# First attention of a two-layer Flamingo block: on TensorE, the scores of even slots are issued in front of the maxima

## Chip, cores and metric

One core of one Trainium2 chip runs the whole kernel. The time is device microseconds from launch to end, the median of three executions.

## What is computed

Two layers follow one another on 16 batches of 112 rows of 256 features: cross attention to 375 context rows and then a mixture of experts, twice. The change lies in the first cross attention, which has 16 heads of 16 features:

```python
q = jnp.einsum('btd,hdk->bhtk', tgt, Wq) + bq[None, :, None, :]
k = jnp.einsum('bsd,hdk->bhsk', src, Wk) + bk[None, :, None, :]
v = jnp.einsum('bsd,hdk->bhsk', src, Wv) + bv[None, :, None, :]
scores = jnp.einsum('bhtk,bhsk->bhts', q, k) * scale
weights = jax.nn.softmax(scores, axis=-1)
out = jnp.einsum('bhts,bhsk->bhtk', weights, v)
```

`tgt` is the normalised x (16 x 112 x 256), `src` the context (16 x 375 x 256).

## The kernel before

The attention takes a batch of 112 query rows at a time. Each of its 16 heads is computed twice. First comes a product of queries by keys whose only use is its row maximum ("maxima", two matmuls for a pair of heads, L400); VectorE reduces it (L782). After four pairs the maxima are turned by TensorE (`turn_maxima`, L410), negated in two parts by VectorE (L787, L789) and put by DMA as two extra rows under the queries. Then the product is computed again, keys by queries, with the maximum already subtracted ("scores", six matmuls, L344). ScalarE takes the exponential of it (L642). TensorE multiplies by the values ("values", L356, four heads at a time), ScalarE copies that result out of PSUM (L637), TensorE turns it back (`turn_values`, L364), and VectorE divides by the sums ("finish", L795 and L797).

A batch is eight slots s = 0 to 7, and each engine has its own `emit` that writes its instructions slot by slot; engines take their instructions in order and meet only at semaphores. In slot s of batch b, TensorE does maxima s of batch b + 1, values in odd slots, and scores s - 2 of batch b (scores 6 and 7 of batch b - 1 in slots 0 and 1). In even slots it also does one of four projections of batch b + 3: keys in slots 0 and 2 (six matmuls), values in slots 4 (twelve) and 6 (six), all recorded at L51. Even slots end with `turn_values`. Batches 13 and 14 have no such projection left, but parts of the output projection; batch 15 has no maxima.

Four waits matter here. Maxima s waits until VectorE has reduced maxima s - 1, because both use the same two PSUM banks (`psMX`). Even scores wait for ScalarE's copy of the values result (`o_copied`), because that result (`psPV`) lies in the first PSUM bank of the even scores. `turn_maxima` waits for an earlier finish of VectorE (`o_free`). The `turn_values` of slots 0 and 4 waits until VectorE has negated the maxima (`turn_free`). VectorE's order in a slot is: reduction; the negation in slots 0 and 4; the low part of the keys (L754) in slots 1 and 3; finish in odd slots.

Of the kernel before, what the change touches and what calls it, by code (L numbers as in the profile page):

```python
# [37 lines left out]
def at_least(engine, sem, value):  # L38

    if isinstance(value, int) and value <= 0:  # L40
        return
    engine.wait_ge(sem, value)
# [68 lines left out]
def ring(b):  # L111
    return Ring(b // 4, b % 4)


def l0_attention(nc, k, a, xd):

    with ExitStack() as ctx:
# [96 lines left out]
        def tail_group(b):  # L214

            return b.b - TAIL if b is not None and isinstance(b.b, int) and b.b >= TAIL else None
# [16 lines left out]
        def scores_at(p, b, s):  # L233

            return (p, s + NJ - LAG) if s < LAG else (b, s - LAG)

        def values_at(p, b, s):

            return (p, 2 + s // 2) if s < 4 else (b, s // 2 - 2)

        def turned_at(p, b, s):

            return (p, 1 + s // 2) if s < 6 else (b, s // 2 - 3)

        def task_at(ws, s):

            if len(ws) == 2:
                return ws[s // 4], s % 4
            return (ws[0], s // 2) if ws and s % 2 == 0 else (None, None)
# [17 lines left out]
        with nc.Block(no_gpsimd_drain=True) as block:  # L267
# [63 lines left out]
            def _(pe):  # L331
                def scores(b, j):

                    if j % JJ == 0:
                        pe.wait_ge(c_in[j // JJ][b.odd], b.half * 64 + 64)
                    at_least(pe, exp_done, b.b * NJ + (j - 1))
                    if j % 2 == 0:
                        at_least(pe, o_copied, b.b * NH + j // 2 - 1)
                    if b.b == 0 and j == 0:
                        pe.wait_ge(v_free, 2 * 3)  # L340
                    for c in range(SC):
                        for h in range(2):
                            side = slice(SIDE * h, SIDE * h + DOT)
                            last = nc.tensor.matmul(psST[:C, j % 2, h, c * T:(c + 1) * T],  # L344
                                                    stkK[side, b.slot, j % JJ, j // JJ, c * C:(c + 1) * C],
                                                    stkQ[side, j % JJ, bass.ds(b.b, 1), j // JJ, :].rearrange("p o q -> p (o q)"),
                                                    start=True, stop=True)
                    last.then_inc(st_full, 1)

                def values(b, g, exps):  # L350

                    pe.wait_ge(exp_done, exps)
                    for c in range(SC):
                        for q in range(QH):
                            h = QH * g + q
                            last = nc.tensor.matmul(psPV[VW * q:VW * (q + 1), :], V[:, b.slot, c, h, :],  # L356
                                                    Pf[:, h // 2 % PB, h % 2, c * T:(c + 1) * T], start=c == 0, stop=c == SC - 1)
                    last.then_inc(pv_full, 1)

                def turn_values(b, g):  # L360

                    pe.wait_ge(o_copied, b.b * NH + g + 1)
                    at_least(pe, o_free, b.b * NH + g)
                    nc.tensor.transpose(k.ps[:T, 6, P:2 * P], oT[:], k.ident[:]).then_inc(o_full, 1)  # L364
# [27 lines left out]
                def maxima(n, j):  # L392

                    if j == 0:
                        pe.wait_ge(k_sp[n.slot], sp_count(n.slot, n.quarter + 1))
                        pe.wait_ge(k_pool[n.slot], pool_count(n.slot, n.quarter + 1))
                    at_least(pe, mx_red, n.b * NJ + j - (1 if n.b == 0 else 0))
                    for h in range(2):
                        side = slice(SIDE * h, SIDE * h + KEYS)
                        last = nc.tensor.matmul(maxima_of(n, j)[:T, h, :S],  # L400
                                                stkQ[side, j % JJ, bass.ds(n.b, 1), j // JJ, :].rearrange("p o q -> p (o q)"),
                                                stkK[side, n.slot, j % JJ, j // JJ, :], start=True, stop=True)
                    last.then_inc(mx_full, 1)

                def turn_maxima(n, half):

                    pe.wait_ge(mx_red, n.b * NJ + JJ * (half + 1))
                    at_least(pe, turn_free, 2 * n.b + half)
                    at_least(pe, o_free, n.b * NH - (3 if half else 5))
                    nc.tensor.transpose(psT[:HH, :], mx[:, n.odd, half].rearrange("p h j -> p (h j)"), k.ident[:T, :T]).then_inc(turn_full, 1)  # L410

                def turn_rows(g, t):

                    pe.wait_ge(o_free, GB * NH * (g + 1))
                    if t == 0 and g == 0:
                        pe.wait_ge(v_free, 2 * B)
                    elif t == 0:
                        pe.wait_ge(y_used, GB * g)
                    elif g < LAST:
                        pe.wait_ge(a_lo, KD * g + 1)  # L420
                    for i in range(GB):
                        last = nc.tensor.transpose(psA(g, t)[:, i * T:(i + 1) * T],
                                                   attn[:, GB * g + i, t * P:(t + 1) * P], k.ident[:T, :T])
                    last.then_inc(a_full, 1)

                def project_rows(n):

                    g, i = n // GB, n % GB
                    if i == 0:
                        pe.wait_ge(w_lo, 4)  # L430
                        pe.wait_ge(a_lo, KD * g + KD)
                    elif g < LAST:
                        pe.wait_ge(y_used, n)
                    three_products(nc, psY(n), [(aT[0][:, g % 2, t, i * T:(i + 1) * T], aT[1][:, g % 2, t, i * T:(i + 1) * T])
                                                for t in range(KD)],
                                   [(wo[0][:, t, :], wo[1][:, t, :]) for t in range(KD)]).then_inc(y_full, 1)
# [44 lines left out]

                def emit(p, b, n, ws, x, l):
                    for s in range(NJ):
                        if n is not None:
                            maxima(n, s)
                        if b is not None and s == 0:
                            turn_maxima(b, 1)
                        of, j = scores_at(p, b, s)
                        row, g = values_at(p, b, s)
                        if row is not None and s % 2 == 1:  # L490
                            values(row, g, row.b * NJ + NJ if of is None else of.b * NJ + j)
                        if of is not None:
                            scores(of, j)
                        if n is not None and s == 4:
                            turn_maxima(n, 0)
                        w, t = task_at(ws, s)
                        if w is not None:
                            (keys if t < 2 else vals)(w, t % 2)
                        o = tail_group(b)
                        if o is not None and s in (0, 2):  # L500
                            turn_rows(o, s // 2)
                        if o is not None and s >= 4:
                            project_rows(GB * o + s - 4)
                        row, g = turned_at(p, b, s)
                        if row is not None and s % 2 == 0:
                            if s == 0 and b is not None:
                                pe.wait_ge(turn_free, 2 * b.b + 2)
                            if s == 4 and n is not None:
                                pe.wait_ge(turn_free, 2 * n.b + 1)
                            turn_values(row, g)  # L510
                    if n is not None and n.b in (GB - 1, Q_TURN - 1):
                        pe.wait_ge(rest_q, 16 * (len(Q_POOL) + (0 if n.b == GB - 1 else len(Q_PIECES))))
                        pe.wait_ge(act_q, 16 * len(Q_ACT))

                emit(None, None, ring(0), (ring(1), ring(2)), None, None)
                for b in range(B + 1):
                    p, b, n, w = (ring(b + d) if 0 <= b + d < B else None for d in (-1, 0, 1, 3))
                    emit(p, b, n, (w,) if w else (), None, None)
# [2139 lines left out]
```

## Time and profile before

| | |
|---|---|
| median of three executions | 891.08 us (890.73 to 892.11) |
| profiled execution | 888.89 us |
| its span, first to last instruction | 886.9 us |
| TensorE busy, of the span | 82% |
| VectorE busy, of the span | 67% |
| ScalarE busy, of the span | 52% |

The profile comes from one execution. The first attention lies in the first third of it: batches 2 to 12 of it run at an even pace between 86.62 us and 237.87 us, 13 and 14 up to 267.47 us. A TensorE row gives the start of a matmul and its modelled end, so the distance between starts is the better measure of what an instruction costs the ones behind it.

### The profile page before, as it was taken

The numbers are of one execution on the slowest core, as the hardware profiler recorded it, in microseconds if no ns is written. First come the engines' busy times: TensorE is split into PE (matmuls) and PEld (weight loads), VectorE is DVE, ScalarE is ACT, GpSimd is POOL, SyncE is SP. The second block draws the span as 40 slices with busy tenths as digits, with TensorE's granted clock in tenths as the row PEclk, the third lists the DMA queues.
The fourth block names the chain that finished last, engine by engine and source line by source line (L and its number), as shares of the span: only waits on it lengthen the run. The fifth ranks groups of instructions, "written<-read, shape, count | busy, mean of one in ns | idle before, by whom it ended". The sixth has DMA issues, their size and how long they took to land. (4 is left out here: it accounts for less than half of the span.)

```text
span 886.9 us, 21023 instructions
## 1 busy us (share of the span) xinstructions
PE 726.0 (82%) x6871; PEld 548.3 (62%) x6871; DVE 594.9 (67%) x1432; ACT 464.7 (52%) x953; POOL 458.5 (52%) x592
## 2 busy tenths in 40 slices
PE   3789999999987598989999998478798379997820
PEld 2456666666665498988777777367686246665510
DVE  5566777777785669884445542678867356667766
ACT  3546666766655468673333331344454247776632
POOL 5788788798600438881000002665833518655555
PEclk9879999999999579999999998797979689999975
DMA  6326444442300428764222223785521214323233
GB/s 174 93 71 148 112 112 118 122 108 74 81 14 2 144 60 295 244 208 129 85 83 79 84 73 89 205 229 166 146 70 44 77 35 139 96 81 95 84 92 104
DMA packets 87662, 98.94 MB, mean 112 GB/s; under 512 B 17260, under 2 KB 77132, under 8 KB 87564
## 3 DMA queue, kind: packets, MB, share of 16 engines
q1 hardware_dynamic: 63468, 66.10, 25.3%
q0 software_dynamic: 16432, 24.66, 10.3%
q10 hardware_dynamic: 7664, 6.89, 2.6%
q8 instruction: 60, 0.98, 0.5%
q14 instruction: 38, 0.31, 0.1%
HBM read 61.03 MB, written 24.38 MB: 96 GB/s over the span
## 5 line engine op out<-in xcount | busy, mean ns | idle before, releaser
L782 DVE TENSOR_REDUCE a_mx<-ps 112x2 f32<-112x750 f32 x128 | 120.2, 939 | 49.9 <-PE ps L400 48.0
L672 POOL DMA_DIRECT2D a_stkK<-a_KS x248 | 119.3, 489 | 19.2 <-issue 14.8
L642 ACT ACTIVATE a_Pf<-ps 125x672 f32<-125x672 f32 x128 | 90.0, 729 | 11.2 <-PE ps L344 9.9
L51 PE MATMUL ps<-f_w2hi,f_hh 128*128 (+1 forms) x292 | 80.3, 275 | 4.0 <-issue 2.8
L51 PE MATMUL ps<-f_w2lo,f_hh 128*128 (+1 forms) x292 | 80.2, 275 | 0.0
L51 PE MATMUL ps<-f_w2hi,f_hl 128*128 (+1 forms) x292 | 80.2, 275 | 0.0
L1841 POOL MEMSET a_half<- 112x2 f32 x1 | 0.1, 94 | 143.7 <-POOLq L88 143.7
L1547 DVE CAST f_hh<-ps 128x512 bf16<-128x512 f32 x41 | 28.4, 692 | 64.4 <-PE ps L1283 64.4
L2453 POOL TENSOR_TENSOR f_rl<-f_rf,f_rh 128x512 bf16<-128x512 f32 x34 | 39.5, 1161 | 59.8 <-DVE f_rh L2521 59.3
L2397 ACT ACTIVATE f_rf<-ps,f_ln 128x128 f32<-128x128 f32 x136 | 54.4, 452 | 25.7 <-PE ps L2348 25.7
L1207 POOL DMA_INDIRECT f_xd<-xn,pos x32 | 54.4, 1700 | 22.9 <-issue 22.9
L51 PE MATMUL ps<-f_w1hi,f_xgThi 128*128 x150 | 57.3, 382 | 0.6 <-DVE f_xgTlo L2502 0.6
L51 PE MATMUL ps<-f_w1hi,f_xgTlo 128*128 x150 | 57.4, 382 | 0.0
L51 PE MATMUL ps<-f_w1lo,f_xgThi 128*128 x150 | 57.4, 382 | 0.0
L400 PE MATMUL ps<-a_stkK,a_stkQ 48*112 48x375 bf16 x256 | 48.6, 374 | 9.9 <-DMA a_stkK<-a_KS 5.4
L1552 DVE TENSOR_TENSOR f_hl<-ps,f_hh 128x512 bf16<-128x512 f32 (+1 forms) x57 | 45.3, 796 | 9.8 <-ACT f_hh L1402 8.9
L356 PE MATMUL ps<-a_Pf,a_V 125*32 125x112 f32 x1536 | 50.6, 265 | 1.4 <-ACT a_Pf L642 1.3
L1388 ACT ACTIVATE f_xgThi<-ps 128x256 bf16<-128x256 f32 x41 | 15.7, 384 | 66.1 <-PE ps L1266 66.1
L344 PE MATMUL ps<-a_stkQ,a_stkK 50*125 50x112 bf16 x768 | 47.2, 228 | 1.2 <-DMA a_stkQ<-a_cneg 0.8
L51 PE MATMUL ps<-f_w2hi,f_rh 128*128 x136 | 37.4, 275 | 8.8 <-POOL f_rl L2453 7.8
L344 PEld LDWEIGHTS ps<-a_stkQ,a_stkK 50*125 50x125 bf16 x768 | 34.2, 134 | 16.0 <-issue 12.0
L356 PEld LDWEIGHTS ps<-a_Pf,a_V 125*32 125x32 f32 x1536 | 35.0, 110 | 13.0 <-issue 8.5
(392 smaller groups left out, 2270.5 us busy)
## 6 DMA issues: line engine op xcount, KB each, us to landing
a_raw<-F_w SPq DMA_DIRECT2D x22, 512.0 KB
f_xg<-f_xd SPq DMA_DIRECT2D x75, 128.0 KB
f_yd<-f_yo SPq DMA_DIRECT2D x75, 128.0 KB
f_raw<-F_w SPq DMA_DIRECT2D x14, 512.0 KB
a_ctxF<-ctxT SPq DMA_DIRECT2D x16, 375.0 KB, 3.5
a_cR<-ctx SPq DMA_DIRECT2D x16, 375.0 KB
a_stkK<-a_KS POOLq DMA_DIRECT2D x248, 23.4 KB, 2.0
f_xd<-a_zero ACTq DMA_DIRECT2D x13, 384.0 KB, 3.2
```

The costliest lines, as they stand in the source:

```text
L51: ins = nc.tensor.matmul(out, l, r, start=first and i == 0, stop=last and i == len(steps) - 1)
L344: last = nc.tensor.matmul(psST[:C, j % 2, h, c * T:(c + 1) * T], stkK[side, b.slot, j % JJ, j // JJ, c * C:(c + 1) * C], stkQ[side, j % JJ ...
L356: last = nc.tensor.matmul(psPV[VW * q:VW * (q + 1), :], V[:, b.slot, c, h, :], Pf[:, h // 2 % PB, h % 2, c * T:(c + 1) * T], start=c == 0, ...
L400: last = nc.tensor.matmul(maxima_of(n, j)[:T, h, :S], stkQ[side, j % JJ, bass.ds(n.b, 1), j // JJ, :].rearrange("p o q -> p (o q)"), stkK[ ...
L642: nc.scalar.activation(Pf[:, j % PB], psST[:C, j % 2, :, 0:SC * T], ACT.Exp, scale=DH ** -0.5).then_inc(exp_done, 1)
L672: pool.dma_start(stkK[SIDE * h + DH * a:SIDE * h + DH * (a + 1), w.slot, jj], KS[2 * DH * jj + DH * h:2 * DH * jj + DH * (h + 1), w.odd, p ...
L782: nc.vector.reduce_max(mx[:, n.odd, j // JJ, :, j % JJ], maxima_of(n, j)[:T, :, :S], AX).then_inc(mx_red, 1)
L1207: nc.gpsimd.indirect_dma_start(out=xd, out_offset=bass.IndirectOffsetOnAxis(pos[:, i, b:b + 1], 0), in_=k.xn[:, b, :], in_offset=None, bou ...
L1547: nc.vector.tensor_copy(like_hidden(s, hh), turned_hidden(s)).then_inc(h_hi, 1)
L1552: tt(like_hidden(s, hl), turned_hidden(s) if s.shared is None else hidden(s), like_hidden(s, hh), ALU.subtract).then_inc(h_lo, 1)
L2397: nc.scalar.activation(rf[:, t % 2, i, :], k.ps[:, 2 + t % 2, i * P:(i + 1) * P], ACT.Relu, bias=ln[:, 1, bass.ds(e, 1), i], scale=ln[:, 0 ...
L2453: nc.gpsimd.tensor_tensor(rl[:, t % 2], rf[:, t % 2], rh[:, t % 2], ALU.subtract).then_inc(r_lo, 1)
```

## The change

Only TensorE's order changes. In slots 0, 2, 4 and 6 the scores, with their waits, are issued first, ahead of the maxima and, in slot 0, ahead of `turn_maxima`. Odd slots keep the order maxima, values, scores.

```diff
                 def emit(p, b, n, ws, x, l):
                     for s in range(NJ):
+                        of, j = scores_at(p, b, s)
+                        row, g = values_at(p, b, s)
+                        if of is not None and s % 2 == 0:
+                            scores(of, j)
                         if n is not None:
                             maxima(n, s)
                         if b is not None and s == 0:
                             turn_maxima(b, 1)
-                        of, j = scores_at(p, b, s)
-                        row, g = values_at(p, b, s)
                         if row is not None and s % 2 == 1:
                             values(row, g, row.b * NJ + NJ if of is None else of.b * NJ + j)
-                        if of is not None:
+                        if of is not None and s % 2 == 1:
                             scores(of, j)
```

On TensorE, at the end of slot 5 and the start of slot 6 of batch 1 (every later batch repeats it), the kernel before has the odd scores, then the maxima, then the even scores, then the projection:

```order
284 L344 MATMUL ps<-a_stkQ,a_stkK 125x112 [waits a0_expdone]
285 L344 MATMUL ps<-a_stkQ,a_stkK 125x112 x5
286 L400 MATMUL ps<-a_stkK,a_stkQ 112x375 [waits a0_mxred]
287 L400 MATMUL ps<-a_stkK,a_stkQ 112x375
288 L344 MATMUL ps<-a_stkQ,a_stkK 125x112 [waits a0_ocopied,a0_expdone,a0_cin11]
289 L344 MATMUL ps<-a_stkQ,a_stkK 125x112 x5
290 L51 MATMUL ps<-a_wv_hi,a_ctxH 125x256 [waits a0_vfree]
```

The changed kernel has at the same place:

```order
284 L344 MATMUL ps<-a_stkQ,a_stkK 125x112 [waits a0_expdone]
285 L344 MATMUL ps<-a_stkQ,a_stkK 125x112 x5
286 L344 MATMUL ps<-a_stkQ,a_stkK 125x112 [waits a0_ocopied,a0_expdone,a0_cin11]
287 L344 MATMUL ps<-a_stkQ,a_stkK 125x112 x5
288 L400 MATMUL ps<-a_stkK,a_stkQ 112x375 [waits a0_mxred]
289 L400 MATMUL ps<-a_stkK,a_stkQ 112x375
290 L51 MATMUL ps<-a_wv_hi,a_ctxH 125x256 [waits a0_vfree]
```

Two scores now stand one behind the other, and the maxima stand behind the wait for ScalarE's copy (`a0_ocopied`). At the start of slot 0 of a batch (here batch 2), before:

```order
303 L400 MATMUL ps<-a_stkK,a_stkQ 112x375 [waits a0_mxred,a0_kinpool3,a0_kinsp3]
304 L400 MATMUL ps<-a_stkK,a_stkQ 112x375
305 L410 MATMUL ps<-ident,a_mx 8x112 [waits a0_ofree,a0_turnfree,a0_mxred]
306 L344 MATMUL ps<-a_stkQ,a_stkK 125x112 [waits a0_ocopied,a0_expdone]
307 L344 MATMUL ps<-a_stkQ,a_stkK 125x112 x5
```

and after:

```order
303 L344 MATMUL ps<-a_stkQ,a_stkK 125x112 [waits a0_ocopied,a0_expdone]
304 L344 MATMUL ps<-a_stkQ,a_stkK 125x112 x5
305 L400 MATMUL ps<-a_stkK,a_stkQ 112x375 [waits a0_mxred,a0_kinpool3,a0_kinsp3]
306 L400 MATMUL ps<-a_stkK,a_stkQ 112x375
307 L410 MATMUL ps<-ident,a_mx 8x112 [waits a0_ofree,a0_turnfree,a0_mxred]
```

Here both the maxima and `turn_maxima` have gone behind the scores.

## Rows read from the trace of the kernel before

**Rows 1.** The page: TensorE's granted clock in 40 slices of the span

```profile
PEclk9879999999999579999999998797979689999975
```

**Rows 2.** Windows: length, busy PE, PEld, DVE, ACT, POOL, PEclk, DMA, GB/s

```profile
86.62:224.30 137.68, 129.95 (x1961) 88.27 (x1962) 105.34 (x221) 93.15 (x172) 116.70 (x215) 1.00 0.42 109
237.87:267.47 29.60, 25.86 (x394) 17.95 (x395) 23.98 (x52) 15.89 (x29) 1.88 (x4) 1.00 0.10 26
```

**Rows 3.** Waits in those ten batches: us in total, times, longest

```profile
DVE a_mx L782 <- PE ps L400: 25.4, 44, 0.9
PEld ps L400 <- DVE a_mx L782: 5.7, 20, 0.4
```

**Rows 4.** Timeline of TensorE, batch 6 (slot 0 at 141.62): start, us

```profile
141.62 0.37 PE L400 MATMUL ps<-a_stkK,a_stkQ 48*112 48x375 bf16 x2
...
143.54 0.27 PE L364 MATMUL ps<-ident,a_oT 128*112 128x128 f32 x1
143.75 0.37 PE L400 MATMUL ps<-a_stkK,a_stkQ 48*112 48x375 bf16 x2
144.04 0.78 PE L356 MATMUL ps<-a_Pf,a_V 125*32 125x112 f32 x24
144.75 0.38 PE L344 MATMUL ps<-a_stkQ,a_stkK 50*125 50x112 bf16 x6
...
146.97 0.37 PE L400 MATMUL ps<-a_stkK,a_stkQ 48*112 48x375 bf16 x2
...
149.43 0.26 PE L410 MATMUL ps<-ident,a_mx 112*8 112x112 f32 x1 [0.50 <-DVE xn L797]
...
151.04 0.37 PE L400 MATMUL ps<-a_stkK,a_stkQ 48*112 48x375 bf16 x2
...
152.44 0.37 PE L400 MATMUL ps<-a_stkK,a_stkQ 48*112 48x375 bf16 x2
152.65 0.33 PE L344 MATMUL ps<-a_stkQ,a_stkK 50*125 50x112 bf16 x6
152.91 0.32 PE L51 MATMUL ps<-a_wv_hi,a_ctxH 128*125 128x256 bf16 x1
...
153.85 0.37 PE L400 MATMUL ps<-a_stkK,a_stkQ 48*112 48x375 bf16 x2
...
155.35 0.37 PE L400 MATMUL ps<-a_stkK,a_stkQ 48*112 48x375 bf16 x2
```

**Rows 5.** Timeline of VectorE, the same batch

```profile
142.03 0.94 DVE L782 TENSOR_REDUCE a_mx<-ps 112x2 f32<-112x750 f32 x1
...
143.17 0.26 DVE L789 SCALAR_TENSOR_TENSOR a_cneg<-ps,a_cneg 8x112 bf16<-8x112 f32 x1
...
145.98 0.93 DVE L782 TENSOR_REDUCE a_mx<-ps 112x2 f32<-112x750 f32 x1
...
149.26 0.94 DVE L782 TENSOR_REDUCE a_mx<-ps 112x2 f32<-112x750 f32 x1
...
152.85 0.94 DVE L782 TENSOR_REDUCE a_mx<-ps 112x2 f32<-112x750 f32 x1
```

**Rows 6.** Timeline, batch 15 (no maxima): values, their copy, next even scores

```profile
269.19 0.78 PE L356 MATMUL ps<-a_Pf,a_V 125*32 125x112 f32 x24
...
270.04 0.26 ACT L637 ACTIVATE a_oT<-ps 128x112 f32<-128x112 f32 x1 [0.23 <-PE ps L356]
...
270.44 0.38 PE L344 MATMUL ps<-a_stkQ,a_stkK 50*125 50x112 bf16 x6 [0.17 <-ACT a_oT L637]
```

**Rows 7.** Timeline of TensorE, batch 0: scores, then maxima

```profile
68.79 0.38 PE L344 MATMUL ps<-a_stkQ,a_stkK 50*125 50x112 bf16 x6
69.01 0.33 PE L400 MATMUL ps<-a_stkK,a_stkQ 48*112 48x375 bf16 x2
```

**Rows 8.** Timeline of TensorE, batch 1, slot 2

```profile
75.65 0.37 PE L400 MATMUL ps<-a_stkK,a_stkQ 48*112 48x375 bf16 x2
...
76.87 0.32 PE L344 MATMUL ps<-a_stkQ,a_stkK 50*125 50x112 bf16 x4 [0.85 <-DMA a_stkQ<-a_cneg]
```

## Prediction

> **What bounds it now.** I began with the windows, because the change touches only the first attention. In the ten batches from 86.62 us TensorE's rows cover 129.95 of 137.68 us and VectorE's 105.34 [rows 2], with TensorE's clock at its full level. So TensorE looks like the limit with VectorE well behind. The chain of waits says more: VectorE stands 25.4 us idle in front of reductions because the maxima have not been computed, and TensorE waits for the reductions as well, 20 times in 80 slots [rows 3]. The two hand one pair of PSUM banks back and forth, maxima, reduction, maxima, and a late link of that loop is late for good unless something else ends later anyway. The timeline of one batch then tells which of the two ends last in each slot [rows 4, 5].
>
> I count from an odd maxima M(o) = 0. The next even maxima stand at 1.40 (151.04 to 152.44) or, in slot 0, at 1.50 (153.85 to 155.35) [rows 4]. From a maxima to its reduction's start it is 0.41 (141.62 to 142.03 and 152.44 to 152.85), and from a reduction's start to the maxima that it releases 0.99 or 1.00 (145.98 to 146.97, 152.85 to 153.85) [rows 4, 5]. The loop's own pace is therefore 1.40 us a slot: the 1.40 above is just this loop, so TensorE, done with the odd scores, waited a little for VectorE.
>
> **What the new order costs.** No instruction is added or removed, and VectorE, ScalarE and the DMA queues keep their order. What moves is the time at which the even maxima start, through two terms.
>
> First, the even scores now come straight behind the odd scores, and so run into the wait for ScalarE's copy of the values result. Before, the maxima covered it. Batch 15 has no maxima and shows the bare sequence: values at 269.19, copy 270.04 to 270.30, even scores at 270.44, which is 1.25 behind the values, 0.17 of it named as waiting for the copy [rows 6]. Values start 0.29 behind M(o) (143.75 to 144.04) [rows 4]; taken as 0.30, the even scores stand at 1.55. Before they stood at 1.61 (151.04 to 152.65) [rows 4]. So going first brings the scores only 0.06.
>
> Second, the maxima follow the scores. The spacing of that pair is seen free of a wait once, 0.22 [rows 7], which puts the even maxima at 1.77, against 1.40 and 1.50: later by 0.37 in slots 2, 4 and 6 and by 0.27 in slot 0. The upper bound of this spacing is 0.40, what is left of 1.40 after 0.29 and the 0.71 from values to odd scores (144.04 to 144.75) [rows 4]; there the maxima also waited for VectorE, so it is surely too much. I take 0.22.
>
> TensorE's own work does not change to speak of. The pair and what follows cost 0.21 + 0.26 before (152.44, 152.65, 152.91) [rows 4]; now 0.22 plus 0.29, the spacing from maxima to a full-array matmul, taken from maxima to values. That is 0.04 more.
>
> What a late even maxima costs differs by slot.
> - Slot 2: its reduction started at 145.98, 2.23 behind M(1) = 143.75 [rows 4, 5], because VectorE was still at the keys and at finish. The late maxima allow 1.77 + 0.41 = 2.18. VectorE still ends last. For TensorE itself the next maxima come at 1.77 + 0.29 + some 1.2 for projection and turn, 3.25 against 3.22 (143.75 to 146.97): +0.03. (The 1.2 is 3.22 less 1.61, 0.26 and about 0.15 of waiting.)
> - Slot 4: the reduction started at 149.26, 2.29 behind M(3) = 146.97 [rows 4, 5]; 2.18 is still in time. The turn of the maxima, which waits 0.50 for finish [rows 4], stays at 149.43, since the late maxima fall into that wait. 0.
> - Slot 6: no such cover, because VectorE has no keys in slot 5. Maxima 1.77, reduction 2.18, slot 7's maxima 3.17 to 3.18, against 2.81 (151.04 to 153.85) [rows 4]: +0.36.
> - Slot 0: from its maxima to the turn of values it is 1.92 (141.62 to 143.54) [rows 4], and that turn waits for reduction and negation (142.03 to 143.43) [rows 5]. Both move with the maxima: +0.27. Everything of slot 1 is queued behind that turn.
>
> A steady batch thus loses 0.36 + 0.27 + 0.03 = 0.66 us. There are eleven of them (2 to 12): 7.3 us. Batch 1 has slots 0 and 6 (0.63) and slot 2, where the scores wait for a DMA until 76.87 while the maxima had gone at 75.65 [rows 8]; now they start about 77.1, their reduction 77.5, slot 3's maxima 78.5, against 76.87 + 0.26 + 1.2 = 78.33: about 0.2, with slot 2's own cost 0.3, together 0.9. Batch 0 loses at slot 6 and gains where its maxima waited for VectorE and scores can now fill the wait: an estimate of +0.3. In batches 13 and 14 output projections stand between odd scores and even maxima in slots 6 and 0, and cover part of the copy: I take batch 13's slot 0 in full, 0.27, and half of the other three, 0.5: 0.8 for both. Batch 15 has no maxima: 0. Sum 7.3 + 0.9 + 0.3 + 0.8 = 9.3 us. The experts start behind a barrier at the end of the attention, so nothing later hides it: the profiled 888.89 becomes 898.2. The median before lies 2.2 higher, and becomes 900.4.
>
> Both ends: with a copy wait that costs nothing (scores about 0.25 behind the odd ones, at 1.25) the even maxima stand near 1.47, slot 6 loses 0.07, slot 0 nothing, and the sum is about 1 us. With 0.40 between scores and maxima each even slot is 0.18 later, slots 2 and 4 lose their cover as well, and 0.66 becomes about 1.25 a batch, 16 to 17 us in all.
>
> **A rule of the skill against this reading.** The Trainium skill, "Perfetto Trace Analysis", section "Identifying the Most-Contended Engine", says that TensorE's matmul busy share misleads and that weight-load busy time is to be set against the occupancy of the others. Rows 2 give 88.27 us of weight load against VectorE's 105.34, so by that rule VectorE is the engine to watch, and it agrees with the loop above. Taken to its end, every delay of a reduction would be paid in full; what that would give is the second rival.
>
> **Rivals.**
> 1. The copy wait is less than batch 15 shows, or VectorE's own lateness covers more slots: +1 to +5 us, 892 to 896. For it: slots 2 and 4 are covered by only 0.05 and 0.11, so small shifts move the balance. Against: batch 15's wait is in the trace, and slot 6 has no cover. 0.13.
> 2. VectorE ends last everywhere: three slots at 0.37 and one at 0.27 are 1.38 a batch, 15.2 over eleven, 2 to 3 more outside: 908.5. For it: the same thin cover. Against: the reductions at 145.98 and 149.26 did not wait for maxima. 0.10.
> 3. The other side, faster: the even maxima's 1.40 is TensorE's own time, not VectorE's, so scores in front fill a gap and nothing waits for the reduction. TensorE's spacing from M(o) to the projection was 1.87; with scores at 1.25, maxima 1.47 and projection 1.76 each even slot gains 0.1, 56 slots 6 us: 885. It decides if even scores come at 1.3 or before. Against: 0.41 + 0.99 is exactly 1.40. 0.06.
> 4. More idle time makes the granted clock fall in the attention. The page's clock digit is 9 from the fourth slice to the twelfth, which is this stretch, also where TensorE is 87% busy [rows 1, 2]. A microsecond at half level costs about as much again; a few such stretches bring 910 or more. 0.04.
> 5. The order hardly matters, within 0.2%, which is also about what a measurement of this kernel can tell from no change: 0.05.
>
> The forecast itself holds 0.62. The likeliest time is 900.4 us; the range 893 to 907.5 takes in most of rival 1 and the upper bound of the spacing, and leaves out rivals 2 to 5 and some of 1. Faster 0.06, same 0.07 (case 5 and the foot of rival 1), slower 0.87.
>
> **What would show it.** In the changed profile: even scores 0.5 to 0.55 behind odd ones, with a wait named for the copy (L637); even maxima near 1.77 behind odd ones; VectorE's idle time in front of reductions up by about 0.6 us a batch; a batch of 14.4 us instead of 13.73 (141.62 to 155.35) [rows 4]; slots 1 to 3 and 3 to 5 as long as before. Even scores at 1.3, or a batch below 13.9, would make the copy term wrong; slots 2 and 4 longer by 0.3 would make the cover wrong; a change of length after the attention would make the barrier argument wrong.

## The result and the profile after

The changed kernel takes 899.89 us (median of 20 executions, 891.34 to 904.91) against 892.18 us (20 executions) of the kernel before: a ratio of 1.0083 with a 95% interval of 1.0066 to 1.0100, or 5.9 to 8.9 us more. The change makes the kernel slower. The forecast was 900.4, 9.3 more than the 891.08 of three executions; measured is a median 7.7 above the 892.18 of twenty. Its profiled execution took 900.16 us, with a span of 898.2, 11.3 more than before.

In the changed kernel the lines of VectorE and ScalarE stand two further down: the reduction is L784, the copy L639, the second negation L791 and finish L799.

The ten batches from batch 2 to batch 11, then a stretch in batch 13 (windows; columns as in the windows of before):

```profile
85.86:228.57 142.71, 127.92 (x1966) 85.29 (x1964) 105.54 (x220) 91.96 (x171) 115.13 (x212) 1.00 0.42 106
245.30:254.80 9.50, 9.49 (x99) 6.33 (x101) 6.42 (x13) 3.87 (x7) 0.00 (x0) 0.50 0.03 6
```

The ten batches took 137.68 us before and take 142.71 now, with about the same work on every engine and TensorE at its full clock level in both [rows 2]. So 0.50 us a batch have come as waiting, not as work. The second row has no counterpart in the windows of before: for 9.5 us in batch 13 TensorE was at its lower level, 1.2 GHz. That is the first part of the difference that the order of instructions does not explain by itself. The page shows it in slice 12:

```profile
PEclk9979999999989669998999999699989688999975
```

The waits of the ten batches (total us, times, longest):

```profile
DVE a_mx L784 <- PE ps L400: 32.0, 60, 1.0
...
PE ps L344 <- ACT a_oT L639: 7.3, 41, 0.7
...
PEld ps L400 <- DVE a_mx L784: 6.2, 20, 0.4
```

VectorE's idle time in front of reductions rose from 25.4 to 32.0 us, and from 44 waits to 60 [rows 3]. TensorE waits for ScalarE's copy in front of 41 of the scores, four a batch and one more.

TensorE's timeline of batch 6 from the maxima of slot 5 to those of slot 7, and behind it slots 0 and 1 of batch 7:

```profile
152.28 0.37 PE L400 MATMUL ps<-a_stkK,a_stkQ 48*112 48x375 bf16 x2
152.58 0.78 PE L356 MATMUL ps<-a_Pf,a_V 125*32 125x112 f32 x24
153.29 0.38 PE L344 MATMUL ps<-a_stkQ,a_stkK 50*125 50x112 bf16 x6
153.84 0.38 PE L344 MATMUL ps<-a_stkQ,a_stkK 50*125 50x112 bf16 x6 [0.17 <-ACT a_oT L639]
154.03 0.35 PE L400 MATMUL ps<-a_stkK,a_stkQ 48*112 48x375 bf16 x2
...
155.41 0.37 PE L400 MATMUL ps<-a_stkK,a_stkQ 48*112 48x375 bf16 x2
...
157.16 0.35 PE L400 MATMUL ps<-a_stkK,a_stkQ 48*112 48x375 bf16 x2
157.44 0.26 PE L410 MATMUL ps<-ident,a_mx 112*8 112x112 f32 x1
...
159.13 0.32 PE L364 MATMUL ps<-ident,a_oT 128*112 128x128 f32 x1 [0.47 <-DVE a_cneg L791]
159.38 0.37 PE L400 MATMUL ps<-a_stkK,a_stkQ 48*112 48x375 bf16 x2
```

The even scores start 0.55 behind the odd ones (153.29 to 153.84), with a wait of 0.17 for the copy. They are 1.56 behind the odd maxima (152.28), 1.55 by the forecast. The maxima follow at 154.03, 1.75 behind the odd ones, 1.77 by the forecast and 1.40 before [rows 4].

VectorE, slots 2, 4, 5, 6 and 7 of the same batch:

```profile
147.23 0.93 DVE L784 TENSOR_REDUCE a_mx<-ps 112x2 f32<-112x750 f32 x1
...
150.51 0.94 DVE L784 TENSOR_REDUCE a_mx<-ps 112x2 f32<-112x750 f32 x1
...
152.69 0.94 DVE L784 TENSOR_REDUCE a_mx<-ps 112x2 f32<-112x750 f32 x1 [0.78 <-PE ps L400]
...
154.42 0.94 DVE L784 TENSOR_REDUCE a_mx<-ps 112x2 f32<-112x750 f32 x1 [0.33 <-PE ps L400]
155.82 0.94 DVE L784 TENSOR_REDUCE a_mx<-ps 112x2 f32<-112x750 f32 x1 [0.47 <-PE ps L400]
```

The reductions of slots 2 and 4, at 147.23 and 150.51, have no wait: VectorE was the later one there, as before. That of slot 6, at 154.42, waits 0.33 for the late maxima and passes the delay on to slot 7 (155.41).

The distances between the starts of maxima, medians over batches 2 to 11, are the most exact measure in this case; where a kernel was profiled twice (before, changed, late_turn), the two agree in each of them to 0.01 us. All kernels of this text in one table (from slot to slot; the last column is the sum, a batch):

| | 0-1 | 1-2 | 2-3 | 3-4 | 4-5 | 5-6 | 6-7 | 7-0 | batch |
|---|---|---|---|---|---|---|---|---|---|
| before | 2.13 | 1.40 | 1.82 | 1.40 | 2.67 | 1.41 | 1.40 | 1.50 | 13.74 |
| changed | 2.11 | 1.74 | 1.48 | 1.77 | 2.30 | 1.74 | 1.39 | 1.74 | 14.27 |
| front_2_4 | 2.12 | 1.74 | 1.48 | 1.77 | 2.30 | 1.41 | 1.41 | 1.50 | 13.73 |
| front_0_6 | 2.11 | 1.40 | 1.82 | 1.41 | 2.67 | 1.74 | 1.39 | 1.74 | 14.27 |
| free_copy_before | 2.31 | 1.41 | 1.81 | 1.41 | 2.67 | 1.40 | 1.49 | 1.50 | 14.00 |
| free_copy_after | 2.21 | 1.41 | 1.81 | 1.43 | 2.65 | 1.41 | 1.49 | 1.50 | 13.90 |
| copy_twice | 2.11 | 1.90 | 1.46 | 1.90 | 2.18 | 1.90 | 1.39 | 1.90 | 14.74 |
| late_turn | 2.13 | 1.41 | 1.82 | 1.40 | 2.18 | 1.63 | 1.41 | 1.50 | 13.48 |
| late_turn_both | 1.73 | 1.57 | 1.82 | 1.41 | 2.17 | 1.64 | 1.41 | 1.50 | 13.25 |
| late_turn_after | 2.11 | 1.74 | 1.48 | 1.77 | 1.94 | 1.74 | 1.39 | 1.74 | 13.91 |

Read it in pairs that begin at an odd slot. From slot 1 to slot 3 it is 3.22 before and after, from 3 to 5 4.07 and 4.07, from 5 to 7 2.81 and 3.13, from 7 to 1 3.63 and 3.85. Slots 2 and 4 lose 0.34 to 0.37 in front of the even maxima and get it all back behind them; slots 6 and 0 do not.

The medians differ by 0.54 a batch, the eleven batches together by 5.7 us and not by 5.9, mainly because batches 3 and 7 were longer than the others already before (13.96 and 14.11) and lose only 0.3 each.

### The profile page after: what moved, and what is told of

Same layout as the page of the kernel before. It is cut to its first block and busy times, and to the rows that moved or that the text cites. A ratio compares the mean times of both kernels' runs of the same rounds, so it can differ in the third digit from the quotient of the medians.

```text
span 898.2 us, 20990 instructions
## 1 busy us (share of the span) xinstructions
PE 723.0 (80%) x6838; PEld 544.4 (61%) x6871; DVE 593.6 (66%) x1432; ACT 463.3 (52%) x953; POOL 460.5 (51%) x592
## 5 line engine op out<-in xcount | busy, mean ns | idle before, releaser
L784 DVE TENSOR_REDUCE a_mx<-ps 112x2 f32<-112x750 f32 x128 | 120.3, 940 | 59.1 <-PE ps L400 58.4
L1209 POOL DMA_INDIRECT f_xd<-xn,pos x32 | 57.0, 1781 | 23.1 <-issue 23.1
L344 PE MATMUL ps<-a_stkQ,a_stkK 50*125 50x112 bf16 x768 | 49.7, 235 | 12.3 <-ACT a_oT L639 9.0
L51 PE MATMUL ps<-f_w1hi,f_xgTlo 128*128 x140 | 54.0, 386 | 1.6 <-DVE f_xgTlo L2504 1.0
L51 PE MATMUL ps<-f_w1lo,f_xgThi 128*128 x140 | 53.4, 382 | 0.5
L356 PE MATMUL ps<-a_Pf,a_V 125*32 125x112 f32 x1536 | 52.7, 273 | 1.3 <-ACT a_Pf L644 1.3
L51 PE MATMUL ps<-f_w1hi,f_xgThi 128*128 x137 | 52.7, 385 | 0.7 <-issue 0.2
L639 ACT ACTIVATE a_oT<-ps 128x112 f32<-128x112 f32 x64 | 16.9, 264 | 59.5 <-PE ps L356 59.5
```

What stands on the lines that cost most here:

```text
L51: ins = nc.tensor.matmul(out, l, r, start=first and i == 0, stop=last and i == len(steps) - 1)
L784: nc.vector.reduce_max(mx[:, n.odd, j // JJ, :, j % JJ], maxima_of(n, j)[:T, :, :S], AX).then_inc(mx_red, 1)
L1209: nc.gpsimd.indirect_dma_start(out=xd, out_offset=bass.IndirectOffsetOnAxis(pos[:, i, b:b + 1], 0), in_=k.xn[:, b, :], in_offset=None, bou ...
```

## Experiments

The theory: the even maxima are held back 0.34 by the scores that wait for ScalarE's copy, and this is paid only in slots 6 and 0, where VectorE has nothing else to be late with. Rivals: the loss is spread over all even slots; or it comes from the pair of scores standing together, not from the copy.

**Only slots 2 and 4 in front.**

```diff
-                        if of is not None and s % 2 == 0:
+                        if of is not None and s in (2, 4):
                             scores(of, j)
...
-                        if of is not None and s % 2 == 1:
+                        if of is not None and s not in (2, 4):
                             scores(of, j)
```

> Only slots 2 and 4 put the scores in front of the maxima; slots 0 and 6 keep the order of before. My theory (the copy wait makes every even maxima 0.34 us late, but in slots 2 and 4 VectorE is still busy with the keys and finish): even maxima there 1.74 behind the odd ones instead of 1.40, and the distances from maxima 1 to 3 and 3 to 5 stay 3.22 and 4.08, so a batch stays at 13.73 and the time within 1.5 us of before. Rival (a late reduction is paid everywhere): both distances 0.34 longer, a batch 14.4, time +8 us or more. Rival (the cost is TensorE's own, of the order scores, scores, maxima): a quarter of the batch's 0.54 in each even slot, so 14.0 a batch and +3.5 us.

Measured: 894.71 us (12 executions) against 894.76 (26), ratio 0.9993 (0.9960 to 1.0025). TensorE's timeline, slots 1 to 4 of batch 6:

```profile
147.09 0.37 PE L400 MATMUL ps<-a_stkK,a_stkQ 48*112 48x375 bf16 x2
...
148.64 0.38 PE L344 MATMUL ps<-a_stkQ,a_stkK 50*125 50x112 bf16 x6 [0.17 <-ACT a_oT L639]
148.83 0.35 PE L400 MATMUL ps<-a_stkK,a_stkQ 48*112 48x375 bf16 x2
...
150.31 0.37 PE L400 MATMUL ps<-a_stkK,a_stkQ 48*112 48x375 bf16 x2
...
152.08 0.35 PE L400 MATMUL ps<-a_stkK,a_stkQ 48*112 48x375 bf16 x2
```

The same wait of 0.17 and the same late maxima (147.09 to 148.83 is 1.74), and slot 3 still comes at 3.22. Two of four even slots can be changed at no price, as the forecast had it.

**Only slots 0 and 6 in front.** The same edit with `(0, 6)`.

> Only slots 0 and 6 put the scores in front. My theory: all of the change's cost is here: maxima 5 to 7 at 3.13 instead of 2.81, maxima 7 to 1 at 3.84 instead of 3.62, a batch 14.27, the time that of the full change, +7 to +9 us over before. Rival (paid everywhere or TensorE's own cost): half of it, a batch 14.0, +4 us.

Measured: 899.21 us (12), ratio 1.0050 (1.0019 to 1.0081). A batch is 14.27, exactly that of the full change. The maxima of slots 5 to 7 of batch 6 lie as in the full change:

```profile
157.59 0.37 PE L400 MATMUL ps<-a_stkK,a_stkQ 48*112 48x375 bf16 x2
...
159.33 0.35 PE L400 MATMUL ps<-a_stkK,a_stkQ 48*112 48x375 bf16 x2
...
160.72 0.37 PE L400 MATMUL ps<-a_stkK,a_stkQ 48*112 48x375 bf16 x2
```

1.74 and then 1.39. So the whole price of a steady batch is in slots 6 and 0; the rival of a spread loss is out. The time itself missed the expectation of +7 to +9: the medians differ by 4.5 us, the interval is 1.7 to 7.2. The 5.7 us of the steady batches lie inside it, but the 7.7 of the full change do not. With the same steady batches the two kernels' rises over before differ by some 3 us, so a median of a dozen executions does not settle the size.

**Without the copy wait, in both orders.** The values result goes to PSUM bank 6, where no scores lie. The even scores then need no wait for the copy. Instead finish, which reads that bank, waits for the copy of the next group, so this costs VectorE something new, and the old order is run with it as the control. The first values of all wait for a negation of the maxima.

```diff
-        psPV = k.ps[:, 0, SC * T:(SC + 1) * T]
+        psPV = k.ps[:, 6, 0:T]
...
-                    if j % 2 == 0:
-                        at_least(pe, o_copied, b.b * NH + j // 2 - 1)
...
                     dve.wait_ge(o_full, b.b * NH + g + 1)
+                    last = isinstance(b.b, int) and b.b == B - 1 and g == NH - 1
+                    dve.wait_ge(o_copied, b.b * NH + g + (1 if last else 2))
```

> The changed order, but the result of values lies in the free columns of PSUM bank 6, so even scores no longer wait for ScalarE's copy (VectorE's finish waits for the copy instead, and the first values wait for the negation). My theory: even scores 0.3 behind the odd ones instead of 0.54, even maxima at about 1.50 instead of 1.74, a batch of 13.8 to 13.95, time +1 to +3 us over before. Rival (the cost comes from the pair's order on TensorE or from three waits in a row, not from the copy): even maxima stay near 1.74 and the time at +7 us or more.

> The same move of the values' result to bank 6 with the order of before: the control for the added waits. My theory: finish starts up to 0.2 us later in slots 5 and 7, which the even maxima cover; a batch 13.7 to 13.85, time -0.5 to +1.5 us against before. Rival (the added waits cost by themselves): +3 us or more, which then has to be taken off the other kernel's time.

Measured in the new order: 900.69 us (9), ratio 1.0084 (1.0050 to 1.0118); in the old order 902.36 (6), 1.0108 (1.0067 to 1.0148). TensorE, slots 5 to 7 in the new order (odd and even scores are now one row of twelve matmuls):

```profile
151.79 0.37 PE L400 MATMUL ps<-a_stkK,a_stkQ 48*112 48x375 bf16 x2
152.09 0.78 PE L356 MATMUL ps<-a_Pf,a_V 125*32 125x112 f32 x24
152.80 0.55 PE L342 MATMUL ps<-a_stkQ,a_stkK 50*125 50x112 bf16 x12
153.20 0.37 PE L400 MATMUL ps<-a_stkK,a_stkQ 48*112 48x375 bf16 x2
...
154.68 0.37 PE L400 MATMUL ps<-a_stkK,a_stkQ 48*112 48x375 bf16 x2 [0.21 <-DVE a_mx L784]
```

The even maxima are back at 1.41 (151.79 to 153.20), although two scores still stand in front of them. So it is the copy wait and not the pair of scores. Without that wait the new order is even the better one: 13.90 a batch against 14.00 of its control. The whole 0.10 is gained between slots 0 and 1 (2.21 against 2.31), where the scores now stand ahead of the waiting `turn_maxima`. It did not make a fast kernel, and here both expectations of the time failed: 5.9 and 7.6 us above before, where +1 to +3 and at most +1.5 had been expected, and the control's batch, 14.00, was expected at 13.85 or less. The wait of finish costs more than I had reckoned: 0.18 between slots 0 and 1 and 0.09 between 6 and 7 in the control, since the turn of the maxima of slot 0, which waits for finish, is in the loop:

```profile
142.74 0.37 PE L400 MATMUL ps<-a_stkK,a_stkQ 48*112 48x375 bf16 x2
143.38 0.26 PE L410 MATMUL ps<-ident,a_mx 112*8 112x112 f32 x1 [0.28 <-DVE xn L799]
```

And from the start of batch 14 to the attention's last turned row it is 35.72 and 34.55 us, against 31.63 before: 4.1 and 2.9 more. The expectation had nothing for this stretch. In the new order 3.4 us of it (260.4 to 263.8) were at the lower clock level, in the old order none; in both the last turns wait up to 1.02 us for finish. With 1.4 and 2.6 in batches 2 to 12 it accounts for 5.5 us of the 5.9 and of the 7.6 by which the two kernels stand above the 894.76 of before. The rest, like all of this, says nothing about the change.

**The copy made later.** In the changed order ScalarE first copies the same result once more into a tile that nobody reads.

```diff
+                            nc.scalar.activation(spare[:], psPV, ACT.Copy)
                             nc.scalar.activation(oT[:], psPV, ACT.Copy).then_inc(o_copied, 1)
```

> The changed order, and ScalarE copies the values' result twice, first into a spare tile, so that the wait of the even scores is about 0.28 longer. It doubles the suspected cost and tells which engine's cover is how deep. My theory: even scores 0.82 behind the odd ones, even maxima 2.02; maxima 1 to 3 at 3.5 instead of 3.22 (TensorE ends last there), 3 to 5 still 4.08 to 4.15 (turn of the maxima waits for finish anyway), 5 to 7 at 3.41 instead of 3.13, 7 to 1 at 4.12 instead of 3.84: a batch of 15.1, time +16 to +20 us over before. Rival (the copy is not what makes the maxima late): a batch stays near 14.3. Rival (no cover at all): 14.27 + 4 x 0.28 = 15.4.

Measured: 907.25 us (4) against 892.04 (17), ratio 1.0210 (1.0156 to 1.0264). ScalarE's timeline at slot 2 of batch 6:

```profile
149.22 0.26 ACT L640 ACTIVATE a_spare<-ps 128x112 f32<-128x112 f32 x1 [1.13 <-PE ps L357]
149.38 0.26 ACT L641 ACTIVATE a_oT<-ps 128x112 f32<-128x112 f32 x1
```

and TensorE's at the same place:

```profile
148.07 0.37 PE L401 MATMUL ps<-a_stkK,a_stkQ 48*112 48x375 bf16 x2
...
149.78 0.38 PE L345 MATMUL ps<-a_stkQ,a_stkK 50*125 50x112 bf16 x6 [0.32 <-ACT a_oT L641]
149.97 0.35 PE L401 MATMUL ps<-a_stkK,a_stkQ 48*112 48x375 bf16 x2
```

The needed copy starts 0.16 later, since the two overlap, not a full 0.26 or more. The wait in front of the even scores goes from 0.17 to 0.32 and the even maxima from 1.74 to 1.90 (148.07 to 149.97): every 0.01 of the copy arrives at the maxima. It is paid as the theory has it, in full in slots 6 and 0 (5 to 7 from 3.13 to 3.29, 7 to 1 from 3.85 to 4.01), nearly nothing in slot 4 (4.07 to 4.08), and in slot 2 from 3.22 to 3.36. There it is TensorE's own work that ends last: before, 0.33 us passed between the start of `turn_values` in slot 2 and the next maxima, 0.12 of it waiting for VectorE; here it is 0.21, the same as in the changed kernel. The change had used this room up, so what came on top was paid. The pattern held. The time, 15.2 us above before, is just under the expected 16 to 20, and the batch of 14.74 is below the expected 15.1, because I had priced the second copy as if it ran alone. The Trainium skill, "ScalarE: Activation LUTs", section "What ACT_TABLE_LOAD costs", has the overlap that I missed: with immediate scale and bias such an instruction takes 186 ns and 0.833 ns an element of each partition, and back to back they overlap by about 93 ns. For 112 elements that is 0.28 less 0.09 = 0.19 of distance, an estimate from these figures, against 0.16 in the trace, which counts.

**Is the rest of the difference the order's?** Each kernel was profiled once more, with no edit.

> The kernel before once more, for a second profile. My theory of the two stretches at half clock inside the attention of the changed kernel (74.7 to 78 us and 245 to 255 us, which its first profile has and the first profile of before has not): they come and go between executions of any of these kernels, so this profile has at least one of them as well, with batch 1 or batch 13 longer by 2 to 4 us, while batches 2 to 12 stay at 13.73. Rival (the change makes the clock fall there): neither here.

> The changed kernel once more, for a second profile. My theory: batches 2 to 12 at 14.27 again; the half-clock stretches may be there or not. Rival (the change causes them): both again, at the same batches.

Measured: 897.15 us before and 897.80 changed, spans 895.5 and 896.1. The parts of the span in both pairs:

| part of the span, changed less before | first pair | second pair | forecast |
|---|---|---|---|
| up to the start of batch 0 | -3.2 | -2.6 | 0 |
| batches 0 and 1 | +2.5 | +4.9 | +1.2 |
| batches 2 to 12 | +5.7 | +5.7 | +7.3 |
| batch 13 | +3.0 | -0.5 | +0.8 for 13 and 14 |
| batch 14 to the end of the attention | +0.5 | 0.0 | |
| after the attention | +2.9 | -7.0 | 0 |
| all | +11.3 | +0.6 | +9.3 |

The eleven steady batches repeat to 0.1 us; nothing else does. Up to the start of batch 0 no changed instruction runs, and still this part took 54.9 and 55.3 us before and 51.7 and 52.7 changed. Over all 13 traces of this study it took 51.7 to 55.3, up to 55.1 with the new order (front_2_4), so the gain of 2.6 to 3.2 is not the order's. The part after the attention, with the same instructions, took 602.4 and 609.6 us before and 605.3 and 602.6 changed. In batch 13 a stretch at the lower clock level came and went in both kernels: it lies in the first profile of the changed kernel (window above) and in the second of the one before, where the mean clock of this window is 0.86:

```profile
238.00:250.00 12.00, 10.42 (x144) 7.32 (x145) 9.08 (x20) 6.52 (x12) 1.88 (x4) 0.86 0.15 40
```

There it made batch 13 longer by 0.8 us (15.81 against 15.02), less than the 2 to 4 expected.

Batch 1 had lasted 14.56 and 14.47 us before, and 17.82 and 20.55 in the changed kernel. TensorE's timeline in batch 1 of the second profile of the changed kernel:

```profile
74.36 0.57 PE L344 MATMUL ps<-a_stkQ,a_stkK 50*125 50x112 bf16 x6 [2.20 <-DMA a_stkQ<-a_cneg]
74.72 0.52 PE L400 MATMUL ps<-a_stkK,a_stkQ 48*112 48x375 bf16 x2
```

and the windows ahead of and behind the wait's end:

```profile
72.00:74.00 2.00, 0.16 (x6) 0.02 (x2) 0.94 (x4) 1.62 (x3) 1.25 (x4) 1.00 0.61 132
74.00:76.00 2.00, 1.64 (x11) 0.92 (x12) 0.72 (x1) 0.73 (x1) 1.33 (x1) 0.50 0.02 3
```

TensorE stands still for 2.2 us because the negated maxima have not landed, and then goes on at half its clock. Is that the new order's? All 13 traces are of one of two kinds. In three (before twice, late_turn once) the clock is low between 66 and 70 us, batch 0 takes 17 us, and the wait in batch 1 is 0.69 to 0.85. In the other ten batch 0 takes 13.6 to 16.4 us, the wait is 1.57 to 3.94, and the low clock lies later than 70 us, in nine of them behind the wait. These ten are all seven of the new order (front_2_4 and front_0_6 among them), and three of the old one. One of these three is late_turn_2nd, the same kernel as late_turn (both are below). Its windows:

```profile
66.00:70.00 4.00, 2.58 (x45) 1.65 (x44) 2.20 (x5) 1.54 (x4) 4.00 (x10) 1.00 0.86 223
74.00:78.00 4.00, 2.09 (x15) 1.12 (x15) 0.57 (x1) 1.77 (x4) 1.60 (x1) 0.85 0.09 22
```

So one and the same kernel shows either kind, and the low stretch is not a thing of the new order alone. Whether the new order makes it likelier is open: seven of seven against three of six is too few to tell. Over whole executions no fall of the clock shows: the mean granted clock of the changed kernel's 20 is 0.917, that of the 26, 17 and 23 executions of before with the other runs 0.915, 0.918 and 0.918.

The wait itself is no good measure of a loss. In all 13 traces it ends 20.9 to 22.4 us behind the start of batch 0, however long batch 0 took; in the first pair at 21.98 and 21.96. A kernel that is through with batch 0 sooner waits longer for a landing at about the same time. What differs lies behind the wait: from its end to the start of batch 2 it is 9.75 and 9.76 us before, 12.24 and 14.78 changed. The forecast's loss for batch 1 is in that, and so is a stretch at the lower clock level, some 3.4 us long in the first profile of the changed kernel and 10 us in the second. How much belongs to either is open.

**The cover of slot 4 taken away, in the old order.** `turn_maxima` of slot 4 waits for finish with everything of TensorE behind it. It is moved behind the projection and `turn_values`; the wait of `turn_values` for the negation goes to slot 6.

```diff
-                        if n is not None and s == 4:
-                            turn_maxima(n, 0)
...
-                            if s == 4 and n is not None:
+                            if s == 6 and n is not None:
                                 pe.wait_ge(turn_free, 2 * n.b + 1)
                             turn_values(row, g)
+                        if n is not None and s == 4:
+                            turn_maxima(n, 0)
```

> The order of before, but in slot 4 turn_maxima is issued behind turn_values instead of in front of the projection (the wait for the negation goes to slot 6). A try at a faster kernel: in slot 4 TensorE waits 0.5 for VectorE's finish at turn_maxima, and again for the negation. My theory: maxima 4 to 5 at 2.15 to 2.2 instead of 2.67, of which VectorE's negation in front of reduction 5 gives back all but 0.2, so a batch of 13.5 to 13.6, time -2 to -3 us. Rival (VectorE alone sets the pace of slots 4 to 6): a batch 13.73, the time within 1 us of before.

> The late turn in slot 4 (order of before elsewhere) timed once more, beside the next two. My theory: batches 2 to 12 at 13.48 again, 0.25 under before, so -3 to -4 us. Rival (the first timing was a lucky set of clock stretches): the batches are 13.48 but the median is within 1 us of before.

Measured: 888.91 us (12), ratio 0.9955 (0.9926 to 0.9984), and again beside the next kernels 887.81 (12) against 891.97 (23), 0.9976 (0.9947 to 1.0005): the first time clear of no change, the second time not quite. From slot 4 to slot 5 it is now 2.18 instead of 2.67, of which 0.22 come back in slot 5 to 6. A batch is 13.48.

**The same in the changed order, and in both halves of the old one.** late_turn_after is the edit above in the changed kernel. late_turn_both makes the same move in slot 0 as well:

```diff
-                        if b is not None and s == 0:
-                            turn_maxima(b, 1)
...
-                            if s == 0 and b is not None:
+                            if s == 2 and b is not None:
                                 pe.wait_ge(turn_free, 2 * b.b + 2)
...
+                        if b is not None and s == 0:
+                            turn_maxima(b, 1)
```

> The changed order with the late turn in slot 4. It takes away the wait of turn_maxima for finish in which the late even maxima of slot 4 are hidden. My theory: maxima 3 to 5 were 4.08 in both kernels; with the late turn they are 3.58 in the old order and 3.65 to 3.75 in the new one, so slot 4 now pays about 0.1 and slots 5 to 6, where the odd scores also precede, lose another 0.1 to 0.3 through the copy; a batch 14.0 to 14.2, time +3.5 to +5.5 us over before and 7 to 9 us over the late turn alone. Rival (slot 4 has cover from another source): a batch 13.48 + 0.54 = 14.02 exactly, the distance 3 to 5 being 3.58.

> The late turn in slot 0 as well: turn_maxima behind the keys and turn_values, the wait for the negation in slot 2. My theory: in slot 0 the next reduction then waits for the negation, which comes later by as much as TensorE is earlier (maxima 0 to 1 at 1.85 to 1.9 instead of 2.13, maxima 1 to 2 at 1.65 to 1.7 instead of 1.41), so a batch 13.45 to 13.55 and the time that of the late turn in slot 4 alone, within 1.5 us. Rival (TensorE's wait for the negation is what counts in slot 0): 13.25 a batch, another -2.5 us.

late_turn_after: 898.15 us (6), ratio 1.0108 (1.0059 to 1.0156). TensorE, slots 3 to 5 of one of its batches:

```profile
179.02 0.37 PE L400 MATMUL ps<-a_stkK,a_stkQ 48*112 48x375 bf16 x2
...
180.79 0.35 PE L400 MATMUL ps<-a_stkK,a_stkQ 48*112 48x375 bf16 x2
...
182.54 0.26 PE L410 MATMUL ps<-ident,a_mx 112*8 112x112 f32 x1
182.73 0.37 PE L400 MATMUL ps<-a_stkK,a_stkQ 48*112 48x375 bf16 x2
```

From slot 3 to 5 it is 3.71 (179.02 to 182.73), against 3.58 in the old order with the same move (1.40 + 2.18). With the waiting `turn_maxima` out of the way the late maxima cost 0.13 in slot 4, where they cost 0.00 before: that wait was the cover. Batch and time both missed the expectation, on different sides: a batch is 13.91, where 14.0 to 14.2 was expected, since slots 5 to 7 lost nothing more (3.13), and the time is 6.2 us above before, where 3.5 to 5.5 was. In the profiled execution batches 1 and 13 took 22.54 and 18.46 us, both with a stretch at the lower clock level, while each steady batch gained 0.36 on the changed kernel.

late_turn_both: 885.77 us (12), ratio 0.9957 (0.9922 to 0.9993). A batch is 13.25, 0.49 less than before. My own expectation for it, 13.45 to 13.55, was wrong and the rival's right. Slots 0 and 1 of batch 6:

```profile
142.64 0.37 PE L400 MATMUL ps<-a_stkK,a_stkQ 48*112 48x375 bf16 x2
142.82 0.36 PE L344 MATMUL ps<-a_stkQ,a_stkK 50*125 50x112 bf16 x6
...
144.08 0.27 PE L364 MATMUL ps<-ident,a_oT 128*112 128x128 f32 x1
144.19 0.26 PE L410 MATMUL ps<-ident,a_mx 112*8 112x112 f32 x1
144.38 0.37 PE L400 MATMUL ps<-a_stkK,a_stkQ 48*112 48x375 bf16 x2
```

The maxima of slot 1 come 1.74 behind those of slot 0, not 2.13, and only 0.17 of it comes back in slot 1 to 2. Two things were in the way before and ended at about the same time: the scores stood behind `turn_maxima`, 0.64 behind the maxima instead of 0.18 now (142.82), and `turn_values` waited for a negation of the same slot. The one edit takes away both, and the runs do not tell them apart. It has the lowest median of this study; that of late_turn, 888.91 and 887.81 in its two sets, lies 2 to 3 us above it; 0.23 a batch gives 2.5.

## Why the prediction was right, and where it was off

- **What bounds it.** Right. The loop of maxima and reduction has a pace of 1.40, and the change moves that loop's link. The same instructions take as long as before; only the waits grew, 25.4 to 32.0 us in ten batches.
- **Term 1, the copy wait.** Right. Forecast 1.55 for the even scores, measured 1.56; free_copy_after took the wait away and the even maxima went back to 1.41, copy_twice made it 0.15 longer and they went to 1.90. Going first brings the scores themselves 0.05 (0.06 forecast).
- **Term 2, scores to maxima.** Somewhat too large: 0.22 taken from batch 1, 0.19 measured (153.84 to 154.03). It enters slots 2, 6 and 0, and so makes 0.09 of the 0.12 by which 0.66 a batch was too high.
- **Where it is paid.** Right in all four slots, shown by front_2_4 and front_0_6: +0.32 in slot 6 (0.36 forecast), +0.22 in slot 0 (0.27), 0.00 in slot 2 (0.03), 0.00 in slot 4 (0). The wait of `turn_maxima` for finish is the cover in slot 4 (late_turn_after). In slot 2 it is VectorE's lateness, together with 0.12 us for which TensorE had waited at the next maxima and which the change uses up.
- **The steady sum.** Forecast 0.66 a batch and 7.3 in all, measured 0.54 and 5.7. It is too high by the 0.12 a batch, 1.3 us, and by batches 3 and 7, which lose only 0.3; the mechanism behind it stands.
- **Batches 0, 1, 13 and 14.** Forecast +2.0 together, measured +5.9 in one pair of traces and +4.4 in the other. These steps are not borne out: batch 1 (0.9) measured +3.3 and +6.1, batch 0 (+0.3) -0.8 and -1.2, batch 13 +3.0 and -0.5. The step for batch 1 has its order right, for the maxima of slot 2 do stand behind the DMA wait (74.72), but both steps reckoned with waits of some tenths at full clock, and the traces show a wait of 2 us for a DMA, and stretches at the lower level that come and go.
- **After the attention: nothing.** The two pairs show +2.9 and -7.0, with no cause in the order, since one kernel differs from itself by as much. The barrier argument is neither shown nor refuted to better than that.
- **The total.** That 900.4 and 899.89 agree to 0.5 us is luck. The median before had moved up by 1.1, the steady batches lost 1.6 less than forecast, and what is left of the medians' 7.7, 2.0 us, happens to be what the forecast had for batches 0, 1, 13 and 14, though in the traces those measured otherwise and the part ahead of batch 0 went the other way.

So 5.7 us are shown, place by place, where the medians differ by 7.7 and the interval begins at 5.9. The 0.2 to 3.2 us that are left are not explained. Batches 0, 1 and 13 are candidates, but the parts ahead of batch 0 and behind the attention differ by as much between executions, and no run separates them.

Of the rivals, "VectorE ends last everywhere" is refuted by front_2_4. The rule of the Trainium skill that the forecast set beside it, "Perfetto Trace Analysis", section "Identifying the Most-Contended Engine", says which engine to work on first and nothing of the size; that every delay would be paid was the forecast's own extension of it. The engine it names was the right one to watch, but occupancy does not tell the price of a late link, which was 0.32 us in one slot and nothing in the next. The rival "faster" took the even maxima's 1.40 to be TensorE's own time. free_copy_after answers it: with scores that wait for no copy the even maxima still come at 1.41, the pace of the loop, so no even slot gains 0.1; only slot 0 does. The clock rival was right in that there are such stretches in the attention; that the change brings them is not shown, and the mean clock does not speak for it. "Less than batch 15 shows" fell: the bare sequence of a batch without maxima gave the wait to 0.01 us.

## What to carry to other kernels

In a loop of two engines that hand one buffer back and forth, an instruction that is moved ahead of the loop's link brings its own waits with it; the link can start only when that wait is over and the moved work is issued, however independent that work is. What it costs is decided slot by slot: find for each which engine ends last, and by how much, and look in the trace for a place where the sequence already runs bare. When the total time scatters by more than the change is worth, the distances between repeated instructions in the steady part, and a kernel with the edit in half of the places, tell what the median can't.

## What the runs showed of the hardware

Stretches of some 3 to 10 us at the lower clock level come and go between executions of one kernel, in batch 0 or 1 and in batch 13. With and without one, batch 13 of the changed kernel took 18.0 and 15.3 us; batch 1 of late_turn, together with a longer wait for a DMA, 18.2 and 14.3. The part behind the attention, with the same instructions, took between 602.4 and 609.6 us in the four traces of the two kernels, and the part ahead of batch 0 between 51.7 and 55.3. The medians of the repeated distances in the steady batches agreed to 0.01 us all the while. And a second copy out of PSUM right behind a first cost ScalarE 0.16 us, though each is shown as 0.26.
